# A Mamba-2 layer on one core: mask rows in three bf16 parts, and the mask products of tile j+2 issued behind the masked product of tile j

## What is computed

```python
A_dt = (dt * A)                                   # per head and token
A_cum = jnp.cumsum(A_dt, axis=-1)                 # within a chunk of 128
L = jnp.exp(_segsum(A_dt))                        # L[l, s] = exp(A_cum[l] - A_cum[s]), s <= l
Y_diag = jnp.einsum('bzlhn,bzshn,bhzls,bzshp->bzlhp', Cc, Bc, L, xch)
Y_off  = jnp.einsum('bzlhn,bzhpn,bhzl->bzlhp', Cc, prev, jnp.exp(A_cum))
Y = (Y_diag + Y_off).reshape(b, s, H, P) + hs * D[None, None, :, None]
g = y * jax.nn.silu(gate)                         # then a group norm and the out projection
```

## Time and profile before

| | |
|---|---|
| median of 3 runs | 1840.83 us (1840.24 to 1841.04) |
| profiled execution, its own time | 1839.37 us |
| span of the profiled execution | 1837.5 us |
| PE busy | 1756.8 us (96%) |
| DVE, ACT, POOL busy | 1307.2, 1011.3, 942.7 us |
| mean granted TensorE clock | 0.986 |

### The profile page before, as it was taken

The page is one execution under the profiler, slowest core; times in us unless marked ns, Lnnn a source line. Parts: engine busy times, 40 slices in busy tenths (PEclk is TensorE's granted clock), DMA queues, the critical chain, the costliest instruction groups (busy, mean ns, idle before and its releaser), DMA issues.

```text
span 1837.5 us, 31116 instructions
## 1 busy us (share of the span) xinstructions
PE 1756.8 (96%) x9656; PEld 1345.4 (73%) x9656; DVE 1307.2 (71%) x2175; ACT 1011.3 (55%) x1706; POOL 942.7 (51%) x721
## 2 busy tenths in 40 slices
PE   6799999999999999999999999999999999999967
PEld 4567777777777777777777777777777777777755
DVE  4766677667866677766776678666777667766788
ACT  6455554655646565665546556465656655565532
POOL 1355464555535565454645555355654546455563
PEclk9999999999999999999999999999999999999988
DMA  6412121121202121121211212121211212111121
GB/s 225 129 33 68 61 67 45 49 64 53 73 28 73 44 72 52 30 73 56 67 46 49 63 53 73 28 73 44 72 52 30 73 56 67 45 54 57 35 98 58
DMA packets 77102, 114.18 MB, mean 62 GB/s; under 512 B 21376, under 2 KB 28032, under 8 KB 76032
## 3 DMA queue, kind: packets, MB, share of 16 engines
q1 hardware_dynamic: 59360, 80.06, 14.4%
q10 hardware_dynamic: 17568, 31.99, 5.3%
HBM read 88.94 MB, written 23.07 MB: 61 GB/s over the span
## 4 chain that ended last, share of the span: by engine, by line
issue 45%; POOL 32%; PE 14%; DVE 4%; ACT 2%; DMA 1%; SPq 1%; POOLq 1%; ACTq 0%; DVEq 0%
POOL yt L1612 9%; POOL ssq L1607 6%; POOL wg_lo L1531 4%; POOL prev L1593 3%; PE bank L478 3%; POOL wx_lo L1531 3%; PE bank L480 3%; PE bank L479 3%; POOL wo_lo L1531 3%; POOL yt L1615 2%; PE bank L653 1%; PE bank L804 1%; PE bank L719 1%; DMA raw_w<-w_in_dram 1%; PE bank L791 1%
## 5 line engine op out<-in xcount | busy, mean ns | idle before, releaser
L1612 POOL TENSOR_TENSOR yt<-yt,ea 128x384 f32<-128x384 f32 (+1 forms) x128 | 189.5, 1480 | 402.0 <-DVE ea L1447 402.0
L1417 DVE TENSOR_TENSOR lm<-lm,cbm 128x512 f32<-128x512 f32 x256 | 186.4, 769 | 178.4 <-ACT lm L1079 178.4
L1225 DVE SCALAR_TENSOR_TENSOR xc<-bank,bpar,xc 128x511 f32<-128x511 f32 (+2 forms) x384 | 285.4, 743 | 6.8
L478 PE MATMUL bank<-h_hi,wg_hi 128*128 128x512 f32 x640 | 263.0, 411 | 22.0 <-ACT gate L1034 12.9
L480 PE MATMUL bank<-h_hi,wg_lo 128*128 128x512 f32 x640 | 251.9, 394 | 0.0
L479 PE MATMUL bank<-h_lo,wg_hi 128*128 128x512 f32 x640 | 251.1, 392 | 0.0
L478 PE MATMUL bank<-h_hi,wx_hi 128*128 128x512 f32 x512 | 210.8, 412 | 2.2 <-DVE bt L1225 2.2
L1593 POOL TENSOR_TENSOR prev<-prev,dec 128x512 f32<-128x512 f32 x96 | 101.9, 1062 | 207.0 <-DVE prev L1363 131.9
L478 PE MATMUL bank<-wo_hi,g_hi 128*128 128x512 f32 x496 | 206.9, 417 | 0.0
L480 PE MATMUL bank<-h_hi,wx_lo 128*128 128x512 f32 x512 | 200.5, 392 | 0.0
L479 PE MATMUL bank<-h_lo,wx_hi 128*128 128x512 f32 x512 | 200.1, 391 | 0.0
(11 more groups left out here) (187 smaller groups left out, 3734.9 us busy)
## 6 DMA issues: line engine op xcount, KB each, us to landing
raw_w<-w_in_dram SPq DMA_DIRECT2D x145, 256.0 KB, 2.7
raw_w<-w_out_dram SPq DMA_DIRECT2D x64, 256.0 KB, 2.6
part_d<-part ACTq DMA_DIRECT2D x64, 256.0 KB, 2.0
part<-part_d ACTq DMA_DIRECT2D x58, 256.0 KB, 2.7
rt<-rows_d SPq DMA_DIRECT2D x256, 8.0 KB
acc<-x_dram SPq DMA_DIRECT2D x8, 256.0 KB, 6.6
acc<-w_mod_dram SPq DMA_DIRECT2D x2, 1024.0 KB, 8.1
lh<-neg_d SPq DMA_DIRECT2D x128, 8.0 KB
```

The costliest lines, as they stand in the source:

```text
L478: nc.tensor.matmul(out_ap, whi(k), hhi(k), start=(k == 0), stop=False)
L1225: stt(dst[:, at], ps[:, 0:HALF - 3 + k], w(k), dst[:, at], ALU.mult, ALU.add)\
L1417: tt(lm[:, h % 4, :], lm[:, h % 4, :], cbm[:, toks(hf)], ALU.mult).then_inc(v_m, 1)
L1612: tt(yt[:, j % 2, cols], yt[:, j % 2, cols], ea[:, j % 2, cols], ALU.add).then_inc(p_t3, 1)
```

## The change

It has two parts. **Rows.** The mask rows, which were held as two fp32r parts, are held as three bf16 parts; a triple's matmuls get 24 rows in place of 16, in bf16. The prologue makes and stores three parts of each row (20 stores in place of 14, each of half the bytes a part), kept in `prev` and `lm`, which are free there. **Order.** Tile 1's triple stays ahead of tile 0; the triple of tile j+2 stands behind the masked product of tile j. ScalarE's and VectorE's orders follow.

```diff
-SROWS = 16
+PARTS = 3
+SROWS = 2 * PARTS + PARTS * NZ + 2 * PARTS
...
-        rt = [sb(f"rt{i}", [128, HALF], R) for i in range(2)]
-        lh = [sb(f"lh{i}", [128, 2 * CHUNK], R) for i in range(2)]
-        sel = sb("sel", [128, 128], R)
+        rt = [sb(f"rt{i}", [128, HALF], BF) for i in range(2)]
+        lh = [sb(f"lh{i}", [128, 2 * CHUNK], BF) for i in range(2)]
+        sel = sb("sel", [128, 128], BF)
...  (TensorE)
                 for j in range(NCT):
-                    if j < NCT - 1:
-                        exp_a(j + 1)
-                        diff(2 * j + 2)
-                        diff(2 * j + 3)
-
                     if j == 0:
+                        exp_a(1)
+                        diff(2)
+                        diff(3)
                         te.wait_ge(v_prev, sb0 + 3)
...
                     lst.then_inc(t_yd, 1)
+                    if j < NCT - 2:
+                        exp_a(j + 2)
+                        diff(2 * j + 4)
+                        diff(2 * j + 5)
                     if j == 0:
                         n = project_step(0, 0)
...  (ScalarE)
-                    if j < NCT - 1:
-                        exp_a(j + 1)
-                        decays(j + 1)
+                    if j == 0:
+                        decays(1)
+                        exp_a(1)
+                        decays(2)
...
+                    if j == 1:
+                        decays(3)
+                    if j < 2:
+                        exp_a(j + 2)
...  (VectorE)
-                    if j < NCT - 1:
-                        mix(2 * j + 2)
-                        mix(2 * j + 3)
+                    if j == 0:
+                        mix(2)
+                        mix(3)
...
+                    if j in (0, 2):
+                        mix(4 + j)
+                        mix(5 + j)
...  (GpSimd, prologue)
-            po.wait_ge(a_row, 1)
-            tt(rows_lo, fx, rows_hi, ALU.subtract).then_inc(p_split, 1)
-            tt(neg_lo, rows_hi, fx, ALU.subtract).then_inc(p_split, 1)
-            po.wait_ge(a_row, 4)
-            tt(flat(wo_lo, 2, 4), fy, flat(wo_hi, 2, 4).bitcast(F), ALU.subtract).then_inc(p_split, 1)
+            po.wait_ge(a_row, 3)
+            tt(fx, fx, row_parts[0], ALU.subtract).then_inc(p_split, 1)
+            po.wait_ge(a_row, 5)
+            tt(fy, fy, exp_parts[0], ALU.subtract).then_inc(p_split, 1)
+            po.wait_ge(p_split, 2)
+            po.wait_ge(a_row, 6)
+            tt(row_parts[2], fx, row_parts[1], ALU.subtract).then_inc(p_split, 1)
+            tt(neg_parts[2], row_parts[1], fx, ALU.subtract).then_inc(p_split, 1)
+            po.wait_ge(a_row, 8)
+            tt(exp_parts[2], fy, exp_parts[1], ALU.subtract).then_inc(p_split, 1)
```

More of the change, by code:

```diff
@@ L252, in adaln_mamba_ffn @@
         PRO_BANK = (7, 0, 1, 2, 3, 7, 0, 1)
+        row_parts = [prev[:, m, :].bitcast(BF) for m in range(PARTS)]
+        neg_parts = [t.bitcast(BF) for t in (prev[:, PARTS, :], prev[:, PARTS + 1, :], lm[:, 0, :])]
+        exp_parts = [lm[:, 1 + m, :].bitcast(BF) for m in range(PARTS)]
         cpad = sq[:, 0:NK * 32].rearrange("p (k n) -> p k n", k=NK)
@@ L311, in unit_params @@
                     two, i, e = slice(q // 2, 4, 2), q % 2, 32 * EA_ROWS[q]
[L312 to L314 removed]
+                    sp.dma_start(rt[p][32 * q:32 * q + 2 * PARTS, :],
+                                 rsrc[two, PARTS * i:PARTS * (i + 1), toks(hf)]).then_inc(d_par[p], 16)
+                    sp.dma_start(rt[p][e + SROWS - 2 * PARTS:e + SROWS, :],
+                                 rsrc[q, 2 * PARTS:4 * PARTS, toks(hf)]).then_inc(d_par[p], 16)
                 nsrc = row(neg_d[hf], nb)
@@ L391, in _ @@
                              small[:, 48 + NZ * f:48 + NZ * (f + 1)]).then_inc(d_scr, 16)
-            sp.wait_ge(p_split, 3)
+            sp.wait_ge(a_row, 6)
+            store_rows(0, 1)
+            sp.wait_ge(a_row, 7)
+            store_neg(1)
+            sp.wait_ge(v_dtt, 4)
+            sp.dma_start(dtw_d.rearrange("b t f w n -> t b (f w n)"),
+                         flat(xdt, 0, 4).rearrange("t (b n) -> t b n", b=NBLK)).then_inc(d_scrt, 16)
+            sp.wait_ge(p_split, 3)
+            store_rows(0, 2)
+            sp.wait_ge(d_scrt, 16)
+            unit_steps(0, 0)
+            pro_fill(8)
+            sp.wait_ge(p_split, 4)
+            store_neg(2)
+            sp.wait_ge(a_row, 8)
             store_rows(1, 1)
+            sp.wait_ge(p_split, 5)
+            store_rows(1, 2)
             sp.wait_ge(a_const, 5)
-            sp.wait_ge(d_scr, 16 * 14)
+            sp.wait_ge(d_scr, 16 * 20)
             unit_params(0, 0)
@@ L982, in _ @@
             pro_split(6)
-            act(flat(g_hi, 0, 2), flat(xw, 0, 2), ACT.Copy).then_inc(a_row, 1)
+            act(row_parts[0], flat(xw, 0, 2), ACT.Copy).then_inc(a_row, 1)
             pro_tap(1)
@@ L986, in _ @@
             se.wait_ge(a_row, 1)
-            act(flat(g_lo, 0, 2), flat(g_hi, 0, 2).bitcast(F), ACT.Copy, scale=-1.0).then_inc(a_row, 1)
+            act(neg_parts[0], row_parts[0], ACT.Copy, scale=-1.0).then_inc(a_row, 1)
             act(flat(yt, 0, 2), flat(xw, 0, 2), ACT.Exp).then_inc(a_row, 1)
             se.wait_ge(a_row, 3)
-            act(flat(wo_hi, 2, 4), flat(yt, 0, 2), ACT.Copy).then_inc(a_row, 1)
+            act(exp_parts[0], flat(yt, 0, 2), ACT.Copy).then_inc(a_row, 1)
             act(small[:, 48:56], flat(yt, 0, 2)[:, CHUNK - 1:TOK:CHUNK], ACT.Copy).then_inc(a_row, 1)
+            se.wait_ge(p_split, 1)
+            act(row_parts[1], flat(xw, 0, 2), ACT.Copy).then_inc(a_row, 1)
+            se.wait_ge(a_row, 6)
+            act(neg_parts[1], row_parts[1], ACT.Copy, scale=-1.0).then_inc(a_row, 1)
             pro_tap(3)
             pro_tap(4)
+            se.wait_ge(p_split, 2)
+            act(exp_parts[1], flat(yt, 0, 2), ACT.Copy).then_inc(a_row, 1)
             keep_row(4)
@@ L1359, in new_state @@
                         ge(ve, t_yo, 4 * u)
+                        if first:
+                            ve.wait_ge(d_scr, 16 * 20)
                         vec.tensor_copy(o, bank[7][:, :]).then_inc(v_prev, 1)
@@ L1676 @@
         for z in range(NZ):
-            rows[32 * q + 4 + z, z * CHUNK:(z + 1) * CHUNK] = 1
-            rows[32 * q + 8 + z, z * CHUNK:(z + 1) * CHUNK] = 1
+            for m in range(PARTS):
+                rows[32 * q + 2 * PARTS + m * NZ + z, z * CHUNK:(z + 1) * CHUNK] = 1
         for i in range(2):
-            cols[32 * q + 2 * i:32 * q + 2 * i + 2, i * CHUNK:(i + 1) * CHUNK] = 1
-            sel[32 * q + 12 + 2 * i:32 * q + 14 + 2 * i, i * 64:(i + 1) * 64] = 1
+            at = 32 * q + PARTS * i
+            cols[at:at + PARTS, i * CHUNK:(i + 1) * CHUNK] = 1
+            at += SROWS - 2 * PARTS
+            sel[at:at + PARTS, i * 64:(i + 1) * 64] = 1
     arrays = {
```

33 lines of the change are left out of this document (11 added, 22 removed).

## The result

The changed kernel takes 1868.44 us (median of 4 runs, 1866.79 to 1870.79) against 1840.53 us (1839.96 to 1841.04) for the kernel before in the same session: a ratio of 1.0156, 95% interval 1.0144 to 1.0168. It is slower by 27.9 us, where 9.3 were forecast; the direction was right and the time lies 1.4 us above the upper end of the range.

What follows compares the result with a forecast made beforehand. The prediction took TensorE to bound the loop; 37 - 12.8 - 12 - 4 + 3.6 - 2.5 = +9.3 us gave 1850 us, slower by 0.5%. Its own case spanned 1844.5 to 1858 (chance 0.62), the range 1841 to 1867.

Steps and rivals of the forecast that it cites:

- wait of the triple of tile 2: Behind tile 0's masked product, TensorE waits for ScalarE's copy of tile 1, 0.82 to 1.77 us a unit: +37 us.
- moved triple: Two triples a unit placed behind the masked product cost 0.43 us in place of 0.63: 64 x 0.20, -12.8 us.
- bf16 triple: bf16 rows shorten each triple's weight load by 0.03 us: -4 us; skill's rule, 11.6 us, not used in the sum.
- clock: Loop keeps full clock, 0 us; rival: half-clock stretches behind the new waits, about 1.7 us each, 1855 to 1877, chance 0.15.
- prologue: More row stores and GpSimd subtractions make the last store and the gate's wait end later: +3.6 us, bounds 0 and 7.
- last unit: VectorE, there the bound, no longer waits for and makes masks ahead of t2: -2.5 us, bounds 0 and -4.6.
- late waits: Most of TensorE's 16.5 us of loop waits for gate, convolution and transposes go: -12 us, bounds 0 and 16.5.
- What comes back later: VectorE's t2 and t1 ahead of masks bring convolution, gating and gate up to 2 us earlier relative to TensorE: -12 us.
- A step that TensorE no longer takes is a gain at once: In the loop, taken as TensorE's: busy 1280.48 of 1300 us, so dropped steps gain and waits in front lose at once.
- All that a better order of the other engines can win in the loop: TensorE's listed loop waits for gate, convolution and transposes, 8.2 + 6.0 + 2.3 = 16.5 us in some 31 units.

Runs made afterwards that it cites:

- run 2: Kernel before with the bf16 rows alone, all three engines in the old order: 1831.29 us, ratio 0.9952.
- run 4: Changed kernel with VectorE in its old order, mask products of the next tile ahead of t2 and t1: 1860.37 us, ratio 1.01.
- run 1: Changed kernel with ScalarE's copy of tile 1's exponentials put back ahead of tile 1's masks: 1819.25 us, ratio 0.9886.
- run 5: Changed kernel with 4, 8, 5 and 4 filling matmuls (c = 0 to 3) in TensorE's wait of every projecting unit: 1856.51 us, ratio 1.0087.
- run 7: Kernel before (fp32r rows, old prologue) with the change's new order on all three engines: 1881.62 us, ratio 1.0225.
- run 10: Kernel of run 1, with GpSimd's sum for tiles 0 and 2 waiting for VectorE's mask products behind t1: 1802.3 us, ratio 0.979.
- run 9: Kernel of run 2, with only TensorE's triple of tile 3 moved behind the masked product of tile 1: 1830.18 us, ratio 0.9936.
- run 3: Changed kernel with eight matmuls, their result overwritten, in TensorE's wait in units with c = 1 only: 1862.85 us, ratio 1.0102.
- run 6: Changed kernel with the changes of run 1 and run 4 together: 1808.17 us, ratio 0.9823.

## Why the prediction was wrong

Term by term, for the profiled executions (the wait of rows 3 to 6 and all else in us):

| term | forecast | measured |
|---|---|---|
| wait of the triple of tile 2 | +37 | +46 from start to start (39.0 in the row of waits) |
| moved triple | -12.8 | -12.8: 64 x 0.20, from 0.52 (rows 2 less 0.11) to 0.32 |
| bf16 triple | -4 | -14: 128 x 0.11, run 2 |
| clock | 0 | +16.4: 10 falls x 1.64, run 4 |
| prologue | +3.6 | +2.8: the gate's wait ends at 94.19, in rows 12 at 91.41 (three row stores, not two, follow the dt table) |
| last unit | -2.5 | -0.9, from its first triple to the end |
| late waits | -12 | about -6 from start to start: -12 behind the masked product of tile 3, +6 ahead of it |

From start to start means summed over the starts of PE's matmuls in the 31 units that project, this trace against that of before. The measured column comes to 31.5.

**The wait** was the right mechanism. By the four kinds of unit it was 0.84, 1.94, 1.31 and 1.03 us in the rows of PE (forecast 0.82, 1.77, 1.13, 1.05), longest with c = 1, and none came ahead of tile 3's triple. What was sized too small is its price. From the masked product of tile 0 to the next projection PE takes 56 us more in all, and 10 of them are the triple itself (31 x 0.32). With c = 0 the projection comes 2.44 us behind the masked product, 1.35 in run 1: 1.09 us for a row of 0.84. Run 1 shows that ScalarE's order of five operations makes the wait.

**The step that failed first is the clock.** The prediction saw the mechanism (rows 14 and 15), named c = 1 and 1.7 us a fall, but took the full clock of the loop under the waits of rows 7 as evidence against it and gave it a chance of 0.15. That evidence was poor: the waits of rows 7 were short ones spread over many places (none in the loop over 0.95 us), and the new one with c = 1 is 1.9 us in one piece. A fall came behind the wait with c = 1 in 8 of 8 groups. Runs 1 and 5 take the idling away in two ways, and the falls go with it; in run 4 one came behind a wait of the same length at another place; run 7 shows that it does not take the bf16 rows.

**"What comes back later" came, and half of it was lost again on VectorE.** The gate did come early, as forecast: 1.1 us of waits in the loop in place of 8.2, and the transposes' 2.3 are gone from the list. But the text moved VectorE's mask products behind t1 and kept their price. Behind t1 they meet GpSimd, take up to 1.78 us each (3.45 for two) in place of 0.69, and the convolution and the masks of tile 3 are late by it: +17.7 us in the two rows of VectorE. From start to start, PE's steps from the masked product of tile 3 to the last gate projection of the next unit are 12 us shorter all the same, and the step to that masked product is 6 us longer (0.88 us a unit with c = 3). Runs 4 and 10 undo the loss from either engine. The Trainium skill, "SBUF — State Buffer", section "SBUF: two separate sides", says that VectorE with two inputs in SBUF and a GpSimd operation that reads SBUF take a shared pair of ports in turns, each for a whole instruction. The trace agrees: 3.45 us for two products beside three operations of GpSimd, 1.28 with GpSimd held back. The prediction did not weigh this rule, and it spoke against the change. Of the convolution's 384 operations at L1248, which take one input from PSUM, the 328 that meet an operation of GpSimd take at most 0.75 us, and so do the 56 that meet none; so it is the product of two SBUF operands that pays.

**The bf16 triple was under-sized,** by 10 us, which hid part of both misses. The prediction put half of the uncovered 0.20 us down to the next product's weight load, which leaves 0.10 that could go, and took 0.03; 0.11 went. The load of the rows fell from 181 ns (rows 9) to 91:

```profile
L677 PEld LDWEIGHTS bank<-rt,lh 24*128 24x128 bf16 x256 | 14.3, 91 | 2.8 <-ACT lm L1094 1.8 <-issue 0.5
```

That is what the Trainium skill, "TensorE: Matmul & The Clock Gate", section "Weight-path perf modes", gave in the prediction (90 ns, 11.6 us as an estimate). The row agrees with it and not with the prediction's doubt. The step to the next product fell by 0.11, a little more than the load; that the load is the whole cause is argued from these two figures, and no run takes it apart from the type of the matmul.

**The bound.** "A step that TensorE no longer takes is a gain at once" is only partly so. With VectorE, ScalarE and GpSimd in the old order, run 2 kept 9.9 of its 14 us and run 9 kept 1 of 6.4; what run 9 lost came back as waits for the gate and the convolution. "All that a better order of the other engines can win in the loop", 16.5 us, was too little: in run 10 the steps from the masked product of tile 3 to the last gate projection are 22.6 us shorter than before. The list of waits shows only time in which no matmul's row is open, and a projection's row is 0.39 us where the next one starts 0.23 behind it. In the kernel before, the gate's projection at 775.32 starts 0.39 behind its forerunner, in the changed kernel 0.23, and the list had no wait there. What run 10 adds to run 1, 17 us, is won on VectorE and GpSimd alone. What stays open is which waits bring a fall: those of run 3 went to c = 3, whose waits are the same in the changed kernel, while longer ones with c = 2 had none. It also stays open how much of the 6 us by which run 10 is ahead of run 6 is the order of VectorE and how much is GpSimd's shorter sums.

## What to carry to other kernels

When an instruction moves past work that used to cover its wait, look at what the other engine does ahead of the release: here the copy behind four operations cost 49 us, and one line gave it back. Where two engines read SBUF, an order also decides what runs beside what: work placed right behind the operation that starts GpSimd is priced from rows beside GpSimd, not from rows alone. And a wait of 1 to 2 us in one place, on an engine that is otherwise always busy, is to be priced with the clock behind it, since another place in the same trace showed that it can fall. A list of waits leaves out what overlapping rows hide; sum the steps from start to start before calling it all that can be won.

## What the runs showed of the hardware

- Filling TensorE's wait with 38 us of useless matmuls made the kernel 11.9 us faster (run 5), because the granted clock then stayed at 2.4 GHz in the loop.
- A wait of 1.9 us was followed by 3.41 us at 1.2 GHz in 8 of 8 units with c = 1 of the changed kernel, and in 5 of 8 in run 4, with the same wait; the executions of run 4 lie 18 us apart. Waits of 1.0 us with c = 3 were followed by one in 1 of 7 units of the changed kernel, in 3 of 7 in run 4 and in 6 of 7 in run 3, and those of 1.3 us with c = 2 in 1 of 8, none and none: the length of the wait alone does not decide it.
- VectorE's product of two SBUF operands (128 x 512, fp32) takes at most 0.69 us when GpSimd does nothing meanwhile and up to 1.78 beside it (1.45 on average in the changed kernel); that one wait on GpSimd saved 17 us.
